# A stack of cross layers on one core: tiles of two rows to a partition, five slots of 4 MB, half of the bias kept in PSUM, and another order of VectorE's work in a pair

## The reference

```
def step(x, wb):
    wi, bi = wb
    xw = jnp.matmul(x, wi)
    x_new = x0 * xw + bi + x
    return (x_new, None)
x, _ = jax.lax.scan(step, inputs, (w, b))
```

## Time and profile before

| what | value |
|---|---|
| median of three runs | 1281.35 us |
| the profiled execution's own time | 1280.2 us |
| its span in the profile | 1278.4 us |
| mean granted TensorE clock | 0.782 |
| VectorE busy | 1150.2 us (90%) |
| TensorE busy (matmul) | 780.7 us (61%) |
| ScalarE busy | 102.7 us (8%) |
| bytes moved | 537.28 MB, 420 GB/s over the span |
| share of the span in the chain that ended last | DMA 72%, VectorE 15%, TensorE 8% |

### The profile page before, as it was taken

How to read it: one execution, slowest core, us unless ns; L and a number is a source line. 1 busy time by engine, 2 the same in 40 slices (tenths; PEclk the granted TensorE clock), 3 DMA queues, 4 the chain that set the end, 5 groups by cost and what they waited for, 6 DMA issues and landing times.

```text
span 1278.4 us, 20057 instructions
## 1 busy us (share of the span) xinstructions
PE 780.7 (61%) x9114; PEld 728.6 (57%) x9114; DVE 1150.2 (90%) x526; ACT 102.7 (8%) x345; POOL 4.3 (0%) x17
## 2 busy tenths in 40 slices
PE   8666666555656655556555665665655665665653
PEld 4666566555556655555545565565655654665653
DVE  5999999898988988989889898898998988989896
ACT  3000000000000000000000000000000000000010
POOL 1000000000000000000000000000000000000000
PEclk9877787887877778778787777777777778678677
DMA  9999999999999999999999999999999999999996
GB/s 385 416 380 428 430 431 431 429 427 429 433 429 431 431 430 432 430 431 424 421 424 425 418 427 421 424 425 422 427 424 421 424 423 425 425 423 425 426 421 286
DMA packets 37385, 537.28 MB, mean 420 GB/s; under 512 B 4168, under 2 KB 4168, under 8 KB 4728
## 3 DMA queue, kind: packets, MB, share of 16 engines
q1 hardware_dynamic: 18432, 268.44, 50.1%
q10 hardware_dynamic: 18936, 268.64, 49.3%
HBM read 268.63 MB, written 268.44 MB: 420 GB/s over the span
## 4 chain that ended last, share of the span: by engine, by line
DMA 72%; DVE 15%; PE 8%; issue 3%; ACT 1%; DVEq 0%
DMA out_dram<-tiles 56%; DMA tiles<-in_r_inputs_dram 15%; DVE tiles L286 8%; DVE blocks L264 7%; PE dots L401 6%; ACT spread L197 1%; PE dots L359 1%; PE scratch L339 1%; DMA tiles<-in_L_rec_w_dram 0%; PE strips L334 0%; PE strips L349 0%; ACT c_last L189 0%; PE turned L370 0%; DVE scale L275 0%; DVEq L42 0%
## 5 line engine op out<-in xcount | busy, mean ns | idle before, releaser
L401 PE MATMUL dots<-blocks,weights 128*64 128x128 f32 x7808 | 662.6, 349 | 380.8 <-DVE blocks L264 380.6
L401 PEld LDWEIGHTS dots<-blocks,weights 128*64 128x64 f32 x7808 | 628.7, 185 | 405.3 <-DVE blocks L264 405.2
L264 DVE STREAM_TRANSPOSE blocks<-tiles 128x2048 f32<-128x2048 f32 x256 | 576.0, 2288 | 100.1 <-issue 100.1
L286 DVE SCALAR_TENSOR_TENSOR tiles<-tiles,scale,c_last 128x4096 f32<-128x4096 f32 (+1 forms) x131 | 571.9, 4368 | 0.2
L197 ACT ACTIVATE spread<-dots,group_mask 128x128 f32<-128x128 f32 (+1 forms) x268 | 75.2, 363 | 1062.6 <-PE dots L401 1020.3
L370 PE MATMUL turned<-layer_sel,spread 128*128 128x8 f32 x512 | 68.1, 258 | 85.5 <-ACT spread L197 85.5
L370 PEld LDWEIGHTS turned<-layer_sel,spread 128*128 128x128 f32 x512 | 62.3, 191 | 101.4 <-issue 95.6
L359 PE MATMUL dots<-blocks,weights 128*64 128x64 f32 x768 | 32.4, 266 | 11.0 <-DVE blocks L264 11.0
L359 PEld LDWEIGHTS dots<-blocks,weights 128*64 128x64 f32 x768 | 31.7, 180 | 12.9 <-issue 12.9
L205 ACT ACTIVATE growth<-turned,ones 128x16 f32<-128x16 f32 (+1 forms) x67 | 18.3, 273 | 85.0 <-PE turned L370 85.0
L275 DVE TENSOR_TENSOR_SCAN scale<-growth,cw 128x6 f32<-128x6 f32 x128 | 13.3, 142 | 8.9 <-ACT growth L205 8.9
(11 more groups left out here) (25 smaller groups left out, 11.3 us busy)
## 6 DMA issues: line engine op xcount, KB each, us to landing
tiles<-in_r_inputs_dram SPq DMA_DIRECT2D x128, 2048.0 KB, 14.9
out_dram<-tiles ACTq DMA_DIRECT2D x127, 2048.0 KB, 25.5
out_dram<-tiles ACTq DMA_DIRECT2D x4, 512.0 KB, 7.0
tiles<-in_L_rec_w_dram ACTq DMA_DIRECT2D x1, 96.0 KB
tiles<-in_L_rec_b_dram ACTq DMA_DIRECT2D x1, 96.0 KB
```

Source lines behind the costliest of these rows:

```text
L264: nc.vector.transpose(blocks[:, p % PLACES, :], source).then_inc(blocks_ready, 1)
L286: nc.vector.scalar_tensor_tensor(out=tiles[:, s, at], in0=tiles[:, s, at], scalar=scale[:, u % 2, t, L - 1:L], in1=c_last[:, at], op0=ALU. ...
L401: last = nc.tensor.matmul(dots[at:at + KM * Q, :, :, :], weights[:, c * CH // Q + k:c * CH // Q + k + KM, :], place[:, :, k * Q:(k + KM) * Q],
```

## The change

- A pair's two rows lie next to each other: row 2p and 2p+1 of a block of 256 go to partition p, so a pair is one transfer of 4 MB with 32 KB per partition, both in and out. The single tiles at both ends stay transfers of 2 MB with 16 KB rows. There are five slots of 4 MB instead of eight of 2 MB, and one load and one store per pair.
- `blocks` has two buffers instead of four, so a transpose waits until TensorE has used the piece two back.
- VectorE transposes all four pieces of a pair, then finishes the second tile of the pair before, then scans this pair and finishes its first tile.
- The bias sum's upper 2048 columns stay in `scratch` in PSUM (`c_high`); only the lower ones are copied to SBUF (`c_low`). `finish` writes each tile in two instructions of 2048 columns. The bias rows are loaded to the partitions 0, 32, 64 and 96 by four DMAs and summed with `ones` of six rows; `of_quarter` and `quarter_sum` are gone.
- ScalarE issues a pair's store after that of the next unit's `make_growth`, once both tiles are done.

```
-PLACES = 4
+PLACES = 2
+PIECES_OF_PAIR = 4
-N_SLOTS = 8
+N_SLOTS = 5
+    x_pairs = x.rearrange("(q p t) d -> q p t d", p=P, t=TB)
+    out_pairs = out.rearrange("(q p t) d -> q p t d", p=P, t=TB)
+    b_halves = b.rearrange("l (h j n) -> j l h n", h=2, j=G)
-        tiles = sb("tiles", [P, N_SLOTS, D])
+        tiles = sb("tiles", [P, N_SLOTS, TB, D])
-        c_last = sb("c_last", [P, D])
+        c_low = sb("c_low", [P, HALF])
+        c_high = scratch[:].rearrange("p j n -> p (j n)")
...
@@ sync
+            for q in range(n_all_pairs):
+                if q >= N_SLOTS:
+                    for t in range(TB if in_singles(q - N_SLOTS) else 1):
+                        sp.wait_ge(y_stored[s][t], 16 * transfers(q - N_SLOTS, t))
...
+                    sp.dma_start(tiles[:, s, :, :], x_pairs[q]).then_inc(x_landed[s][0], 16)
@@ scalar
-            keep_bias(0)
-            spread_dots(0)
-            keep_bias(1)
+            act.wait_ge(bias_summed, 1)
+            nc.scalar.copy(c_low[:], c_high).then_inc(c_low_ready, 1)
...
             for u in range(1, n_units):
...
+                spread_dots(u)
+                make_growth(u)
+                store(u - 1)
@@ vector, finish
-                parts = 1 if n < n_tiles - 1 else PIECES
+                parts = 2 if n < n_tiles - 1 else STORE_PARTS
...
+                    c = c_low[:, at] if i < parts // 2 else c_high[:, i * width - HALF:(i + 1) * width - HALF]
@@ vector, loop over the units
                 wait_tiles(u)
-                transpose_pieces(u, range(2))
+                transpose_pieces(u, range(2 * n_of))
...
-                scan(u - 1)
-                finish(u - 1, 0)
+                if n_before == 1:
+                    scan(u - 1)
+                finish(u - 1, n_before - 1)
                 if n_of == TB:
-                    transpose_pieces(u, range(2, 2 * TB))
-                for t in range(1, n_before):
-                    finish(u - 1, t)
+                    scan(u)
+                    finish(u, 0)
```

More of the change, by code:

```diff
@@ L120, in tiles_of, with in_singles, transfers @@
             return u + n_pairs * (TB - 1), 1
+        def in_singles(q):
+            return q * TB < HEAD or q * TB >= n_tiles - TAIL
         def pieces_before(u):
             return 2 * tiles_of(u)[0]
+        def transfers(q, t):
+            return sum(1 for k in range(q % N_SLOTS, q + 1, N_SLOTS) if t == 0 or in_singles(k))
         def weights_of(g):
@@ L215, in _ @@
             act.wait_ge(cw_all_ready, 1)
             nc.scalar.copy(cw[:], strips[:, 0, 0:LP]).then_inc(cw_ready, 1)
+            spread_dots(0)
             make_growth(0)
             for u in range(1, n_units):
[L219 to L230, removed]
@@ new lines, in _ @@
+                make_growth(u)
+                store(u - 1)
+            last_slot = (n_all_pairs - 1) % N_SLOTS
+            for i in range(STORE_PARTS):
+                at = slice(i * D // STORE_PARTS, (i + 1) * D // STORE_PARTS)
+                act.wait_ge(tiles_done, n_tiles + i)
+                act.dma_start(out_pairs[n_all_pairs - 1, :, TB - 1, at],
+                              tiles[:, last_slot, TB - 1, at]).then_inc(y_stored[last_slot][TB - 1], 16)
+            for q in range(n_all_pairs - N_SLOTS, n_all_pairs):
+                s = q % N_SLOTS
+                act.wait_ge(y_stored[s][0], 16 * transfers(q, 0))
+                if transfers(q, 1) > 0:
+                    parts = STORE_PARTS if q == n_all_pairs - 1 else 1
+                    act.wait_ge(y_stored[s][1], 16 * (transfers(q, 1) - 1 + parts))
@@ L285, in finish @@
                     at = slice(i * width, (i + 1) * width)
-                    nc.vector.scalar_tensor_tensor(out=tiles[:, s, at], in0=tiles[:, s, at],
-                                                   scalar=scale[:, u % 2, t, L - 1:L], in1=c_last[:, at],
-                                                   op0=ALU.mult, op1=ALU.add).then_inc(tiles_done, 1)
+                    c = c_low[:, at] if i < parts // 2 else c_high[:, i * width - HALF:(i + 1) * width - HALF]
+                    done = nc.vector.scalar_tensor_tensor(out=tile[:, at], in0=tile[:, at],
+                                                          scalar=scale[:, u % 2, t, L - 1:L], in1=c,
+                                                          op0=ALU.mult, op1=ALU.add)
+                    if parts == STORE_PARTS or i == parts - 1:
+                        done.then_inc(tiles_done, 1)
             dve.wait_ge(w_copied, W_BANKS)
@@ L338, in sum_bias @@
                 for j in range(G):
[L339 to L344 removed]
+                    if h == 0:
+                        pe.wait_ge(b_landed[j], 16)
+                    last = nc.tensor.matmul(scratch[:, j, :], ones[j * Q:j * Q + L, :], b_rows[j * Q:j * Q + L, h, :],
+                                            start=True, stop=True, tile_position=(j * Q, 0))
+                last.then_inc(bias_summed, 1)
+            pe.wait_ge(ones_ready, 1)
             sum_bias(0)
+            pe.wait_ge(strips_b_landed, 16)
             pe.wait_ge(earlier_built, L)
@@ L395, in _ @@
                 pe.wait_ge(dots_spread, n * G + (HEAD - 1) * G)
-                for c in range(PLACES):
-                    pe.wait_ge(blocks_ready, n * PLACES + c + 1)
-                    place = blocks[:, c, :].rearrange("p (t n) -> p t n", t=TB)
+                for c in range(PIECES_OF_PAIR):
+                    pe.wait_ge(blocks_ready, n * PIECES_OF_PAIR + c + 1)
+                    place = blocks[:, c % PLACES, :].rearrange("p (t n) -> p t n", t=TB)
                     for k in range(0, CH // Q, KM):
```

112 lines of the change are left out of this document (48 added, 64 removed).

## The result

The changed kernel takes 1333.99 us (median; 1331.6 to 1336.18, 4 runs) against 1281.49 us before (1281.14 to 1282.9, 4 runs): a ratio of 1.0407, 95% interval 1.0388 to 1.0427. It was forecast at 1337 us in a range of 1306 to 1354. The profiled execution has a span of 1332.2 us.

A forecast was written before the change was run, and what follows sets the result against it. Transfers bound the old kernel, VectorE close behind; after the change a serial chain would. Span 35.5 + 61 x 20.45 + 51.7 = 1334.7 us, with the profiled run's offsets 1337 us, 4.4% slower; range 1306 to 1354.

The forecast's parts named there:

- The chain and its period: Within a pair, transposes, last matmuls, spread, turn, growth, scan and first finish run one after another: 20.45 us a pair.
- fourth transpose: VectorE's last transpose of a pair waits for TensorE's second piece and starts 6.31 us after the pair's first matmul.
- The burst of 6.27 us for the two first pieces: TensorE starts each pair at half clock after a pause of about 7.5 us; its first two pieces take 6.27 us.
- both covers go: New order and two buffers remove VectorE work that hid TensorE's lateness: a 4.4 us finish, and 5.1 us before the scan.
- Finish in halves, bias from PSUM: VectorE's finish in two halves takes 4.53 us in place of 4.40; reading bias from PSUM costs nothing, at most 0.1 a half.
- Larger transfers: Loads and stores with 32 KB packets gain 0.9% (0 to 1.8%), 19.65 us a pair, below 20.45, so they give nothing.
- third rival: First two pieces run at full clock, transfers stay the bound and larger packets pay: 1270 us, or 1255; chance 0.06.
- Ends: Before and after the pairs: first pair's transposes at 35.5 us, 1.1 us less; last part 51.7 us in place of 55.8.
- Tail: Four single tiles in the old order after the last pair, to the end of the span: 51.7 us, before 55.8.
- The marks that were named: Signs in the later profile: period near 20.45 us, DMA share about 0.95 at 410 GB/s, VectorE waits about 2 us a pair.

The follow-up runs named there:

- far rows: Changed kernel with VectorE's old order and a partition's two rows 128 rows apart in memory: 1281.87 us with one transfer a pair, 1288.01 us with two.

## Why the prediction was right, step by step

**The chain and its period: right in mechanism and in size.** Forecast 20.45 us a pair, measured 1247.04 / 61 = 20.44: 18.35 in the first pair, 20.48 from the eighth on. The steps behind it, forecast and measured from the first matmul of a pair (609.12): fourth transpose 6.31 and 6.34; its piece 8.67 and 8.71; spread 10.69 and 10.72; scan 13.35 and 13.39; next transposes 18.1 and 18.12. The order and the two buffers made the loss (1332.5 us with no change to tiles, transfers and finish), and the half clock was its cause (1290 with TensorE kept busy).

**The burst of 6.27 us for the two first pieces: right value, thin reason, and some luck.** I took it because the pause would be longer than any before. The length of the pause doesn't fix it: with a pause 0.22 us longer the stretch at half clock was 0.47 us shorter (4.85 in place of 5.32), and start and clock settle, here at 20.48 us. From the rows alone any value between 20.05 and 20.8 could have come out, so that it came within 0.03 of 20.45 was luck in part; that one period then holds in every pair wasn't foreseen.

**The two buffers.** The text named them and the order together as what removes the cover. Four buffers with the new order take 1288 us, so in this order the buffers carry most of the loss, and in the old order none. Put as "both covers go", this was right; the text had not priced one without the other.

**Finish in halves, bias from PSUM.** Forecast 4.53 a finish, measured 622.71 to 627.24 = 4.53. PSUM costs under 10 ns a half.

**Larger transfers: the term that was mis-sized, and hidden.** I took 0.9% from the rate of 4 KB against 16 KB packets, with bounds 0 and 1.8%. Where the transfers bound the kernel, the first half moves 431 GB/s against 430 (0.2%) and the second 410 against 424 (3% less), so the whole is 0.9% slower and not faster: outside the bounds. It did no harm to the forecast since the chain hid it, but the third rival's 1270 us was out of reach: with the clock held up it comes to 1290. (Its 1255 takes the 1.2% between 425 and 430 GB/s off the whole run; off half of it that is 7 us, so 1263.) The fixed cost that I read off the rows doesn't show in packets above 16 KB: far rows in one transfer move 431 GB/s in the first half too. What I left out is that the same change puts other rows next to each other in memory. The Trainium skill's "DMA: Bandwidth & Descriptors" ("Where 436 GB/s comes from") gives a ceiling of 435.2 GB/s for the SBUF ports; the best stretch of 400 us of any run here is 432, so the traces agree with that ceiling.

**Ends.** First pair's transposes at 35.56 (forecast 35.5). Tail 1332.2 - 1282.60 = 49.6 against 51.7: the steps between single tiles are 8.91 and twice 9.11 as reckoned (8.95, 9.15), the last scan comes 10.80 after its transposes in place of 9.92, and from there to the end it is 11.7 us in place of 14.5. The work is the same in both, a 2 MB store issued 1.8 us ahead of the last four of 512 KB. It landed in 6.3 us in place of 9.3, and they in 5.9 in place of 7.0 (median); why isn't shown.

**The marks that were named.** Waits of VectorE for TensorE of 2 us a pair (1.59 + 0.30 + 0.24) and the period came as written. The DMA share didn't: 0.99 where 0.95 was forecast, with the rate at 410 as forecast. From 200 to 600 us the packets of the changed kernel took as much of the engines' time for 164.6 MB as those of the old order did for 172.5 MB, so the share doesn't tell how near the transfers are to their limit; why the packets took longer isn't shown.

## What to carry to other kernels

Before work is regrouped on the busiest engine, ask what its old order covered: here a 4.5 us instruction stood between an engine's output and its need for another engine's answer, and moving it cost 4% with two buffers and 0.5% with four. Price the covered engine at the clock that it starts with after its pause (0.50 here after 2.9 us and after 7.4 us), and count the buffers together with the order. A transfer's efficiency is judged by its rate in a run that it bounds, not by the busy share, and an edit to a layout changes which addresses are neighbours as well as the packet's size.

## What the runs showed of the hardware that was not expected

- A loop whose length hangs on TensorE's clock can settle: 20.48 us in every pair, the same with 0.27 us more work in it; with 0.94 us more it goes round in cycles of seven or eight pairs, 20.96 on average.
- 14 added matmul records a pair, 7.95 us of TensorE's time, made the kernel 44 us faster (1334 to 1290) by holding the clock at 0.95 from 100 to 500 us and 0.92 after that.
- Transfers slow down in the second half of the run, in the kernel before too (430 to 424 GB/s); with rows 2p and 2p+1 in one partition, one transfer a pair, the drop is larger (431 to 410), whichever half of the rows is taken then.
- DMA engines show a busy share of 0.99 at 409 GB/s and of 1.00 at 431 GB/s with the same transfers.
- With 2 MB transfers and far rows, storing and loading each tile as soon as it can be, in place of both tiles of a pair together, was worth 0.5% (0.9995 against 1.0052).
